# Row maxima of a whole unit at once in two of eight attention jobs, byte masks on ScalarE instead of VectorE, and new instruction orders

## The reference

```python
x = layernorm(x + attn0(x, Wq, Wk, Wv, Wo))       # 32 heads of 8, 8 kv heads
x = layernorm(x + ffn0(x, gate_w, up_w, down_w))  # weights rounded to float8_e4m3fn, per-column scales
x = layernorm(x + attn1(x, wq, wk, wv, wo))       # 16 heads of 16, 8 kv heads
x = layernorm(x + ffn1(x, lut[gate_idx], lut[up_idx], lut[down_idx]))  # 16-entry table, inner width 688
# attn: softmax(q k^T / sqrt(dh)) v Wo        ffn: (silu(x Wg) * (x Wu)) Wd
```

## Time and profile before

| what | value |
|---|---|
| time, three runs | 332.85, 336.48 (median), 337.21 us |
| the profiled execution's own time | 333.81 us |
| its span, first to last instruction | 331.6 us |
| mean granted clock of TensorE | 0.943 |
| PE busy | 300.7 us, 91% |
| DVE busy | 255.1 us, 77% |
| ACT busy | 234.9 us, 71% |
| POOL busy | 199.4 us, 60% |

### The profile page before, as it was taken

How to read it: one execution, slowest core, us unless ns; L and a number is a source line. 1 busy time by engine, 2 the same in 40 slices (tenths; PEclk the granted TensorE clock), 3 DMA queues, 4 the chain that set the end, 5 groups by cost and what they waited for, 6 DMA issues and landing times.

```text
span 331.6 us, 7198 instructions
## 1 busy us (share of the span) xinstructions
PE 300.7 (91%) x2608; PEld 208.8 (63%) x2608; DVE 255.1 (77%) x472; ACT 234.9 (71%) x432; POOL 199.4 (60%) x273
## 2 busy tenths in 40 slices
PE   8555877879899999999999999999999999999993
PEld 7331333324444557678666776877879778879992
DVE  7699998999999999999985987577666744535253
ACT  2768689999997768776967966886685656564340
POOL 5876443562448489696887675655564322847664
PEclk9895768599799999999999999999999999999997
DMA  4563442153302054100320050364041000000001
GB/s 134 142 190 116 130 123 74 54 140 86 112 6 65 19 138 125 36 29 3 82 65 5 16 144 14 107 191 148 3 107 38 2 1 4 32 3 32 2 2 63
DMA packets 24889, 23.07 MB, mean 70 GB/s; under 512 B 3558, under 2 KB 24854, under 8 KB 24854
## 3 DMA queue, kind: packets, MB, share of 16 engines
q1 hardware_dynamic: 24854, 22.61, 23.7%
HBM read 10.47 MB, written 3.26 MB: 41 GB/s over the span
## 4 chain that ended last, share of the span: by engine, by line
PE 69%; DVE 20%; issue 5%; POOL 3%; ACT 1%; POOLq 0%; DVEq 0%; ACTq 0%
PE FB L1301 17%; PE PV L1244 12%; PE MM L1188 9%; PE FB L1330 8%; DVE MX L988 8%; DVE LV L1104 6%; PE SC L1223 4%; PE FB L1273 4%; PE SC L1218 4%; PE FB L1140 3%; PE FB L1256 2%; POOL LV L753 2%; PE FB L1282 2%; DVE QS L941 1%; PE MM L1320 1%
## 5 line engine op out<-in xcount | busy, mean ns | idle before, releaser
L869 ACT ACTIVATE PB<-SC 128x1024 f32<-128x1024 f32 x96 | 98.0, 1021 | 27.8 <-PE SC L1218 14.6
L988 DVE TENSOR_REDUCE MX<-MM 128x2 f32<-128x512 f32 x128 | 81.0, 681 | 4.8 <-PE MM L1188 3.9
L1188 PE MATMUL MM<-KS,QS 62*128 62x256 bf16 (+1 forms) x384 | 58.9, 287 | 15.0 <-DVE MX L988 11.9
L992 DVE TENSOR_REDUCE MX<-MM 128x4 f32<-128x1024 f32 x32 | 39.1, 1221 | 21.9 <-PE MM L1188 21.9
L1244 PE MATMUL PV<-PB,VP 128*32 128x256 f32 x768 | 52.8, 401 | 0.0
L735 POOL TENSOR_TENSOR HL<-HF,HH 128x256 fp32r<-128x256 f32 (+1 forms) x48 | 36.5, 771 | 24.6 <-ACT HH L846 24.5
L1188 PEld LDWEIGHTS MM<-KS,QS 62*128 62x128 bf16 (+1 forms) x384 | 24.4, 97 | 42.6 <-DVE MX L988 28.1
L1104 DVE COPY_PREDICATED LV<-LB,LV 128x1728 f32<-128x1728 uint8 (+2 forms) x30 | 41.2, 1373 | 3.5 <-POOL LV L753 3.1
L1301 PE MATMUL FB<-XH,W 128*128 128x256 f32 x192 | 43.0, 305 | 0.0
L753 POOL TENSOR_SCALAR LV<-LB,LD,LT 128x432 f32<-128x432 uint8 x56 | 38.8, 706 | 1.6 <-DVE LB L1088 0.7
L1301 PE MATMUL FB<-XL,W 128*128 128x256 f32 x192 | 38.5, 282 | 0.0
(11 more groups left out here) (108 smaller groups left out, 597.4 us busy)
## 6 DMA issues: line engine op xcount, KB each, us to landing
QS<-QP SPq DMA_DIRECT2D x48, 128.0 KB, 2.4
IX<-in_idx SPq DMA_DIRECT2D x10, 216.0 KB, 3.3
dw<-LO SPq DMA_DIRECT2D x10, 216.0 KB, 2.2
W1L<-dw SPq DMA_DIRECT2D x10, 216.0 KB, 2.8
KS<-KP SPq DMA_DIRECT2D x24, 64.0 KB, 2.0
XT<-in_xt SPq DMA_DIRECT2D x4, 256.0 KB, 3.1
X<-in_x SPq DMA_DIRECT2D x4, 256.0 KB, 3.0
KS<-KP SPq DMA_DIRECT2D x24, 32.0 KB, 1.9
```

What stands on the lines that cost most here:

```text
L869: act.activation(PB[:, quad % PB_QUADS, kt, :, :], SC[:, :, :], ACT.Exp, scale=DH[layer(j)] ** -0.5).then_inc(exp_done, 1)
L988: dve.tensor_reduce(mx[:, f, :], MM[:, 2 * f:2 * f + 2, :], axis=AX.X, op=ALU.max).then_inc(max_red, 1)
L992: dve.tensor_reduce(mx, MM[:, :, :].rearrange("p (f i) s -> p f i s", f=2), axis=AX.X, op=ALU.max).then_inc(max_red, 2)
L1188: ins = pe.matmul(MM[:, 2 * f + i, :], QS[lo:lo + r, j % NST, qs + h, qt * P:(qt + 1) * P], keys(j)[lo:lo + r, j % NST, ks, :], start=True ...
```

## The change

1. `by_bank(j)` is true only for jobs 0 and 1. In jobs 2 and 3 PE now waits for the whole unit before, and DVE makes one reduction (L992's form) instead of two (L988's) in each of 32 units.
2. The byte mask `BIG` is made by ACT, by an `Abs` with scale 0.25 from the quarter-scaled bytes into unsigned bytes, between the two casts to bytes and the two casts back. DVE's AND and its semaphore `big_done` go. ACT no longer waits for `big_done` ahead of a chunk; it now waits for `q8_used` (DVE's masked copy of the chunk before) right after `q8_done`, ahead of the `Abs`. DVE waits only for `q8_cast`.
3. All five lists of `ORDER` are rewritten. They hold the same steps as before.

```diff
 def by_bank(j):
-    return layer(j) == 0
+    return j < 2
...
     "ACT": (
-        "lutix.0 q.0 kv.0 qmid.0 kmid.0 lut1.0.2 lut1.0.3 lutix.1 q8.0 lutlow.0 q.1 q8.1 lutix.2 qmid.1 kv.1 lut1.1.2 "
+        "lutix.0 q.0 kv.0 qmid.0 lutix.1 lut1.0.2 lut1.0.3 kmid.0 q8.0 q.1 lutlow.0 q8.1 qmid.1 lut1.1.2 lut1.1.3 q8.2 "
...
     "DVE": (
-        "lutbits.0 scales lut2.0 lut3.0 lut4.0 q8.0 lutbits.1 max.0.0 max.0.1 max.0.2 max.0.3 q8.1 max.0.4 lut2.1 q8.2 "
+        "scales lutbits.0 lut2.0 lut3.0 lut4.0 q8.0 lutbits.1 max.0.0 max.0.1 max.0.2 max.0.3 q8.1 max.0.4 lut2.1 q8.2 "
...
-        "max.1.15 mt.1.1 lut4.5 max.2.0 wo.0 max.2.1 max.2.2 q8.11 lutbits.6 max.2.3 max.2.4 turn.1.0 max.2.5 max.2.6 "
+        "max.1.15 mt.1.1 lut4.5 max.2.0 wo.0 max.2.1 max.2.2 lutbits.6 q8.11 max.2.3 max.2.4 turn.1.0 max.2.5 max.2.6 "
...
-        "max.3.8 mt.3.0 lut2.8 lut3.8 max.3.9 turn.2.0 max.3.10 lut4.8 max.3.11 turn.2.1 max.3.12 down.1 max.3.13 "
+        "max.3.8 mt.3.0 lut2.8 lut3.8 max.3.9 turn.2.0 max.3.10 lut4.8 max.3.11 turn.2.1 max.3.12 down.1 lutbits.9 "
+        "max.3.13 max.3.14 max.3.15 wo.2 mt.3.1 max.4.0 max.4.1 max.4.2 max.4.3 lut2.9 gu.2.0 gu.2.1 max.4.4 gu.2.2 "
...
     "PE": (
+        "score.1.5 max.1.15 max.2.0 mt.1.1@0 score.1.6 pv.1.1.0 pv.1.1.1 score.1.7 max.2.1 pv.1.1.2 score.1.8 max.2.2 "
+        "pv.1.1.3 score.1.9 max.2.3 tr.0.0@1 score.1.10 max.2.4 turn.1.0@2 score.1.11 max.2.5 gu.0.0.0@0 gu.0.0.1 "
...
-        big_done = sem("big_done")
...
                     if c >= 1:
                         act.wait_ge(q8_cast, c)
-                        act.wait_ge(big_done, c)
                     act.activation(Q8A, RAW[:, c % 2, :], ACT.Copy, saturate=False)
                     act.activation(Q8B, RAW[:, c % 2, :], ACT.Copy, scale=0.25, saturate=False).then_inc(q8_bytes, 1)
                     act.wait_ge(q8_bytes, c + 1)
                     if c >= 1:
                         act.wait_ge(q8_done, c)
+                        act.wait_ge(q8_used, c)
+                    act.activation(BIG[:, :], Q8B, ACT.Abs, scale=0.25)
                     act.activation(QA, Q8A, ACT.Copy)
                     act.activation(QB, Q8B, ACT.Copy, scale=4.0).then_inc(q8_cast, 1)
...
                     c = step[1]
-                    dve.wait_ge(q8_bytes, c + 1)
-                    if c >= 1:
-                        dve.wait_ge(q8_used, c)
-                    dve.tensor_scalar(BIG[:, :].bitcast(I32), Q8B.bitcast(I32), 0x40404040, None,
-                                      ALU.bitwise_and).then_inc(big_done, 1)
-                    dve.wait_ge(big_done, c + 1)
                     dve.wait_ge(q8_cast, c + 1)
                     dve.copy_predicated(QA, BIG[:, :], QB).then_inc(q8_used, 1)
```

## The result

The changed kernel takes 341.42 us (median of four runs, 339.92 to 342.50), the kernel before 336.61 beside it (332.85 to 337.21). The ratio is 1.0212 with a 95% interval of 1.0158 to 1.0265: slower, clear of no change though not clear of the 2% bound, where I had forecast slightly faster. The profiled execution took 342.50 us, with a span of 340.3.

What follows compares the result with a forecast made beforehand. The end was taken as the moment PE's list becomes dense, plus unchanged PE work. Early −0.6, whole-unit maxima 0, shapes −0.5 made −1.1 us: 332.7 profiled, 335.4 beside the median of 336.48; range 331.0 to 341.5.

Steps and rivals of the forecast that it cites:

- the second rival: Early stretch, to 97 us: ACT becomes the bound through the added Abs, +4.0 us, so 340.5; chance 0.25.
- they hold the same steps: All lists: PE's work changes only by shape changes between steps, 126 in the old list, 122 in the new; −0.5 us.
- the lists' shuffling near the start: SP's loads moved past each other near the start, where PE waits for DVE anyway; counted at nothing.
- The early stretch: Up to 97 us: −1.4 before 50 us, +0.5 from 50 to 97, +0.3 at the start, together −0.6 us.
- The mask: Weight chunks: DVE loses 0.24 us each, ACT gains 0.41; −1.4 us before 50 us, +0.5 from 50 to 97.
- The handoff: Jobs 2 and 3: DVE idles 0.46 us where two whole-unit maxima follow each other; taken as 0 for the end.
- the cover is DVE's 4.1 us: Jobs 2 and 3: DVE's 4.1 us of idle time absorbs its list getting about 0.8 us longer; 0 for the end.
- the third rival: Jobs 2 and 3: waits between whole-unit maxima make DVE the bound, +7.1 us, so 343.6; chance 0.12.
- the seven pairs: Jobs 2 and 3: max steps following each other directly in DVE's new list, 0.46 us idle each, +3.2 us on DVE.
- Changes of shape: PE's list from max.2.0 on: fewer switches between steps of unlike tile shape, 122 instead of 126, −0.5 us.
- Start: Very start: scales ahead of lutbits.0 on DVE gives POOL and ACT the first table bits later, +0.3 us.
- The table rival: Chunks after 50 us: ACT reloads its function table for Abs, 15.4 us, so about 351; chance 0.03.

Runs made afterwards that it cites:

- e1: Kernel before with only the five rewritten lists, mask on DVE and maxima by bank as before: 1.0105 of the kernel before.
- e11: Kernel before with whole-unit maxima in job 3 only, lists and mask of before: 1.0008 of the kernel before; profiled execution 336.92 us.
- e9: Changed kernel with the mask by ACT for the first six chunks only and by DVE for the last six: 1.0209 of the kernel before.
- e5: Changed kernel with max.0.12 moved ahead of q.3.0 and max.0.13 ahead of two pv steps in PE's list: 1.0126 of the kernel before.
- e2: Kernel before with only the mask moved to ACT, lists and maxima as before: 1.0032 of the kernel before.
- e4: Kernel before with both code edits (mask on ACT, whole-unit maxima in jobs 2 and 3) but the old lists: 1.0070 of the kernel before, 337.5 us.
- e10: Kernel before with the mask by ACT for the first six chunks only, lists and maxima of before: 0.9940 of the kernel before, 333.36 us.
- e6: Changed kernel with 13 unread identity products added in PE's gaps of job 0: 1.0113 of the kernel before, 338.17 us.
- e12: The changed kernel run again, without further edits: 1.0195 of the kernel before.
- e8: Changed kernel with the maxima of jobs 2 and 3 by bank again, new lists and mask on ACT kept: 1.0111 of the kernel before.
- e13: Kernel before with only the new lists, plus 13 unread products in PE's gaps of job 0: 1.0163 of the kernel before.
- e15: Changed kernel with maxima by bank again and 13 unread products in PE's gaps of job 0: 1.0107 of the kernel before.
- e7: Kernel before with 13 unread products added in PE's gaps of job 0: 0.9999 of the kernel before, 335.08 us.
- e14: Kernel before with the mask by ACT for the first six chunks and 13 unread products in job 0: 0.9967 of the kernel before.

## Why the prediction was wrong

I forecast a gain of 1.1 us, and the medians show a loss of 4.8. That 341.42 us still lies inside my range is luck: its upper end, 341.5, was set by the second rival's 340.5, and that rival covers only a part of what happened.

**The step that failed most: "they hold the same steps", and that the lists' shuffling near the start counts "at nothing".** I priced the lists by PE's changes of tile shape alone and put their early part at zero because "PE waits for DVE anyway". It was the other way round there. In the changed kernel DVE waits for PE behind `kv.2.1`, `q.3.0` and two `pv` steps, of which only `q.3.0` stood ahead of `max.0.12` before, and since the clock is at 1.2 GHz in that stretch these take 2 us each. The last sentence of my prediction named a projection delayed near the start as a way to fail, but gave it no price. The lists alone are 1.05% (e1). In job 0's second half the clock accounts for about 2.0 of the 3.15 us (e11 against before, the same code, 2.0; e9 against the changed kernel, the same lists, 2.07), and the order for about 1.1 (e5; e9 against before at the same clock, 1.08). The early stretch, forecast at −0.6 us, came to +5.35 at mt.1.1, and to +2.92 against e11's profile, in which the kernel before has the low clock as well.

**The mask: right in mechanism, half wrong in size.** Up to 50 us I forecast −1.4 us; e2 shows −1.32 at mt.0.0 and −1.75 at mt.0.1. From there to mt.1.1 I had +0.5; e2's profile takes 41.11 us instead of 38.59, +2.5, but e4's, with the same code up to there, 38.92, +0.3. From mt.0.1 to mt.1.0 the clock is 0.71 in e2, 0.82 in e4 and 0.81 before, so e2's excess is not the mask's alone. Both reach mt.1.1 0.7 to 0.8 us late. An Abs costs 30.03 − 29.60 = 0.43 us on ACT, as the casts do, so the price was right. That the room was missing, as the second rival said for this stretch, shows in the chain from 50 to 97 us, where I had named ACT as its sign. Here it is by line for e4, then for before:

```profile
by line: ACT PB L868 31.3%; issue 14.7%; ACT LV L916 12.8%; ACT AA L891 6.2%; ACT TH L898 5.7%; ACT HF L899 5.5%; ACT AA L892 5.4%; ACT BIG L897 4.5%; PE SC L1212 1.7%; ACT MP L808 1.5%; ACT ON L875 1.4%; ACT WF L830 1.3%; ACT VP L785 1.1%;
```

```profile
by line: DVE LV L1104 22.2%; issue 19.5%; DVE MX L988 18.7%; PE MM L1188 6.5%; POOL LV L753 5.9%; PE PV L1244 5.8%; POOL QR L696 2.5%; POOL W L691 2.4%; DVE LB L1088 2.4%; PE FB L1273 2.3%; POOL LO L742 2.3%; PE SC L1218 1.8%; PE FB L1256 1
```

The view cuts each line at its end. ACT's exponentials, look-up steps, casts and masks lead e4's chain, and no line of ACT is among those shown of before's. With the mask on ACT for six chunks only, e10's chain there has 2.2% of exponentials and the kernel gains 0.6%; for all twelve it gains nothing (e2). The two starts of the Abs's price are from ACT's timeline of the changed kernel:

```profile
29.60 0.52 ACT L897 ACTIVATE BIG<-AA 128x384 uint8<-128x384 fp8e4 x1
30.03 0.51 ACT L898 ACTIVATE TH<-AA 128x384 f32<-128x384 fp8e4 x1
```

**The handoff: "the cover is DVE's 4.1 us" was a mean over two jobs.** The mechanism was the third rival's, with the place wrong. Busy time by stretch of the kernel before, in the columns of the earlier trace rows, from mt.1.1 to mt.2.1 (job 2) and from there to mt.3.1 (job 3):

```profile
95.89:131.34 35.45, 33.68 (x346) 19.78 (x348) 34.33 (x69) 27.55 (x45) 26.79 (x38) 1.00 0.29 82
131.34:172.36 41.02, 41.02 (x431) 27.96 (x424) 38.09 (x74) 30.82 (x55) 32.45 (x40) 1.00 0.16 43
```

So DVE had 1.1 us to spare in job 2 and 2.9 in job 3, and five of the seven pairs stand in job 2. A handoff also costs 0.59 us of DVE idle, not 0.46, as DVE's timeline of the changed kernel shows:

```profile
106.23 1.23 DVE L992 TENSOR_REDUCE MX<-MM 128x4 f32<-128x1024 f32 x1 [0.59 <-PE MM L1182]
...
110.16 1.23 DVE L992 TENSOR_REDUCE MX<-MM 128x4 f32<-128x1024 f32 x1 [0.59 <-PE MM L1182]
```

Five of them make 2.9 us, and PE, whose next `max` waits for a whole unit, stands still for 4.1 us in job 2:

```profile
PE MM L1182 <- DVE MX L992: 4.1, 7, 1.3
```

Take off 16 x 0.075 us for the shorter reductions and 0.24 for the AND that is gone, and 1.5 us are left; e6, whose DVE has these five waits and only 0.27 us more, takes 36.96 us for job 2, 1.5 more than before. In the changed kernel's profile another 1.0 us comes from one copy of the look-up, which took 0.64 us before:

```profile
121.45 1.64 DVE L1098 COPY_PREDICATED LV<-LB,LV 128x432 f32<-128x432 uint8 x1
```

Why it is longer there is not shown. e12 (38.00 us) and e4 (38.14) have further waits of DVE for PE in its place. Forecast 0, measured +1.5 (e6) to +2.9 (e9) in job 2, of which the five handoffs explain 1.5. In job 3 it is +0.4 with the old lists (e11) and nothing with the new: 41.32 and 41.30 us by bank (e1, e8), 41.34 in whole units.

**Changes of shape.** Forecast −0.5 us from `max.2.0` on. From mt.1.1 to the end, the new lists take 236.59 to 237.00 us with all maxima by bank (e1, e8, e13, e15), the old ones 235.71 to 236.32 (before, e2, e7, e10, e14): no gain, but a loss of 0.3 us or more. Counting transitions was no good measure of a full PE list.

**Start.** `scales` ahead of `lutbits.0` was put at +0.3; mt.0.0 came 0.27 later in the changed kernel, though the mask should have brought 1.3 there, and 0.4 later with the lists alone (e1). The price is not shown, though: with the same code up to there mt.0.0 comes at 39.33 us in the changed kernel and at 38.47 in e8, at 39.06 before and at 39.68 in e11.

**The table rival** did not occur: one load of 1.283 us in the changed kernel, as in the one before. This agrees with the Trainium skill ("ScalarE: Activation LUTs", section Table sets: the hidden batching unit), by which abs is among the functions that every set holds.

**What stays open.** Job 1's second half takes 22.2 to 24.0 us in every kernel with both the new lists and the mask on ACT, against 21.3 and 21.6 with the lists alone and 20.3 and 21.0 with the mask alone (e4, e2). Neither by bank (e8), nor half of the masks (e9), nor the products (e6, e15) took it away. It is no small piece: against e11's profile, with the old lists and the low clock, the changed kernel loses 2.70 us there, 2.24 in job 2 and 1.15 in job 0's second half. The time goes with the clock of that stretch: with the new lists 21.30 us at 1.00 (e1), 22.22 and 21.61 at 0.92 (e5, e13), 22.91 and 22.89 at 0.85 (after, e8) and 23.96 at 0.81 (e6). At 1.00 the old lists take 20.26 (e4), so about 1.0 us looks like the order's and the rest like the clock's. But no run set the clock there, at 0.92 the old lists take no longer than at 1.00 (20.21 and 20.28 in e11 and e14), and whether the clock brings the waiting there or the waiting the clock is not shown. What makes the clock come up in some executions of the kernel before and in none of the eight of the changed kernel (0.916 to 0.922 in the mean of each) was not found either.

## What to carry to other kernels

Price a new order of steps like a new instruction: list which long step now stands ahead of each step that the full engine waits for, and take its duration at the clock that the stretch has. Slack has to be read job by job; a mean over two jobs hid that the first had hardly any. Moving an instruction to another engine paid here only in the stretch where that engine had room, and it can be moved for that stretch alone.

## What the runs showed of the hardware

The same code took 18.24 us at a clock of 0.60 and 0.74 and 20.24 us at 0.50, from one execution to the next (before, e11): 2.0 of the 3.1 us between the two (333.81 and 336.92 us). Thirteen products that nobody reads, put where PE waits, narrowed that kernel's runs from 332.8 to 337.0 down to 333.75 to 335.60 us (e7), but in e13 the same products left the clock at 0.50 and 0.67. An Abs from fp8 bytes to unsigned bytes runs at the pace of the casts, 0.43 us for 128 x 384.
